# Cross-attention on Trainium2: a rearranged step, and the shift and the subtraction of the maxima as products of 32-row strips

## What is computed

```python
qk = einsum('bhqd,bhkd->bhqk', Q, K)
scores = qk / sqrt(dk)
mean_sim = scores.mean(axis=(-2, -1))
max_sim = scores.max(axis=-1).mean(axis=-1)
probs = softmax(scores)
entropy_proxy = var(probs, axis=-1, ddof=1).mean(axis=-1)
feats = stack([mean_sim, max_sim, entropy_proxy], axis=-1)
hidden = gelu(linear(feats, w1, b1))
hidden = gelu(linear(hidden, w2, b2))
log_t = clip(linear(hidden, w3, b3), log(0.1), log(10))
t = exp(log_t)[..., None]
attn = softmax(qk / (2.0 * t))
return linear(einsum('bhqk,bhkd->bhqd', attn, V), Wo, bo)
```

## Time and profile before

| | us |
|---|---|
| median of 3 runs | 1907.29 (1903.29 to 1908.61) |
| profiled execution | 1907.09 |
| its span, first to last instruction | 1905.3 |
| TensorE busy | 1729.3 (91%) |
| VectorE busy | 1236.1 (65%) |
| ScalarE busy | 923.1 (48%) |
| GpSimd busy | 835.5 (44%) |

### The profile page before, as it was taken

How to read it: one execution, slowest core, us unless ns; L and a number is a source line. 1 busy time by engine, 2 the same in 40 slices (tenths; PEclk the granted TensorE clock), 3 DMA queues, 4 the chain that set the end, 5 groups by cost and what they waited for, 6 DMA issues and landing times. The chain is left out here.

```text
span 1905.3 us, 42459 instructions
## 1 busy us (share of the span) xinstructions
PE 1729.3 (91%) x14484; PEld 1286.7 (68%) x14484; DVE 1236.1 (65%) x2802; ACT 923.1 (48%) x2143; POOL 835.5 (44%) x815
## 2 busy tenths in 40 slices
PE   1999999999947799988999898999699999999998
PEld 0455555555525566666666565555599999999998
DVE  4666666766624566677557666511687777887776
ACT  1455555555423345565556556432455445455543
POOL 1433343344334365666547566411244334444332
PEclk9999999999965578999789898755699999999999
DMA  5000000000000000000000000000000000000000
GB/s 156 2 2 2 1 1 1 1 1 1 2 5 5 4 6 5 6 7 7 5 5 6 5 7 5 2 1 1 1 9 7 8 8 8 8 7 6 8 8 12
DMA packets 26230, 16.50 MB, mean 9 GB/s; under 512 B 6099, under 2 KB 23445, under 8 KB 26133
## 3 DMA queue, kind: packets, MB, share of 16 engines
q1 hardware_dynamic: 26132, 15.23, 2.9%
HBM read 9.97 MB, written 4.19 MB: 7 GB/s over the span
## 5 line engine op out<-in xcount | busy, mean ns | idle before, releaser
L803 ACT ACTIVATE xa_P<-xa_SK 77x1024 f32<-77x1024 f32 x128 | 130.6, 1020 | 161.3 <-PE xa_SK L1088 161.3
L280 ACT ACTIVATE sa_P<-sa_SK 128x1024 f32<-128x1024 f32 x128 | 131.2, 1025 | 147.1 <-PE sa_SK L423 147.1
L246 POOL TENSOR_TENSOR sa_KM<-sa_HQK,sc_headmask 128x512 fp32r<-128x512 f32 x64 | 66.5, 1039 | 292.2 <-ACT sa_HQK L275 292.2
L1361 POOL TENSOR_TENSOR ff_zz<-ff_zt 128x256 f32<-128x256 f32 x32 | 38.3, 1197 | 319.9 <-DVE ff_zt L1558 319.9
L739 POOL TENSOR_TENSOR xa_QMH<-xa_QBH,xc_headmask 128x512 fp32r<-128x512 f32 x64 | 72.0, 1126 | 220.0 <-ACT xa_QBH L795 220.0
L1429 ACT ACTIVATE ff_SG<-bank 128x512 f32<-128x512 f32 x128 | 76.7, 599 | 189.1 <-PE bank L1631 188.9
L1548 DVE TENSOR_TENSOR ff_GL<-ff_GU,ff_GH 128x512 fp32r<-128x512 f32 x128 | 147.4, 1170 | 28.6 <-ACT ff_GH L1434 28.4
L353 DVE TENSOR_REDUCE sa_mx<-sa_SQ 128x8 f32<-128x1024 f32 x128 | 156.6, 1223 | 6.8 <-PE sa_SQ L423 5.4
L1696 PE MATMUL bank<-fh_r,ff_GH 128*128 128x256 f32 x512 | 148.3, 290 | 0.0
L1629 PE MATMUL bank<-ff_ZH,fh_b 128*128 128x256 f32 x512 | 147.7, 288 | 0.0
L1630 PE MATMUL bank<-ff_ZL,fh_b 128*128 128x256 f32 x512 | 144.9, 283 | 0.0
(11 more groups left out here) (254 smaller groups left out, 5430.9 us busy)
## 6 DMA issues: line engine op xcount, KB each, us to landing
xa_shift<-xa_row SPq DMA_DIRECT2D x256, 2.0 KB
out<-X SPq DMA_DIRECT2D x64, 64.0 KB, 1.6
xa_cx<-ctx SPq DMA_DIRECT2D x64, 38.5 KB
sa_shift<-sa_mT SPq DMA_DIRECT2D x64, 8.0 KB, 1.8
fr_b<-L_ffn_B SPq DMA_DIRECT2D x2, 256.0 KB, 3.9
fr_r<-down_a SPq DMA_DIRECT2D x1, 512.0 KB, 4.7
fr_w<-L_ffn_w_gate SPq DMA_DIRECT2D x1, 256.0 KB, 3.4
fr_w<-L_ffn_w_up SPq DMA_DIRECT2D x1, 256.0 KB, 3.6
```

The source lines that it names most:

```text
L280: nc.scalar.activation(P[:, 2 * (k % 2) + h, :], SK[:], ACT.Exp).then_inc(p_ready, 1)
L803: nc.scalar.activation(P[0:TC, (2 * b + h) % 4, :], SK[0:TC, :], ACT.Exp).then_inc(p_ready, 1)
```

## The change

In the part of the cross-attention alone:

- The maxima of the 16 heads are spread over 96 columns (MX: 6 at 0, 6 at 32, 4 at 64), so that mT has the maxima of each bank of SQ in rows of a 32-row group of their own, and subtract_max multiplies 32 rows for each bank.
- The product of pick and shift in by_key takes 32 rows instead of 128. row has 96 partitions and goes to shift by five DMAs (PIECES) instead of four.
- project moves from behind scores_inner to the head of TensorE's step, writes M instead of R, and adds the bias as a product of two fp32r rows (high and low part) with minus ones. residual moves to the head of DVE's step. o_transpose waits for onT_sb of the batch before instead of x_done.
- The MLP writes its three layers into the last quarter of R. POOL makes the features (similarity once a round, variance every second step), DVE the reciprocals (inverse_sums) every second step; the upper clip is done on the exponential. A round's step no longer defers the transposes and qkv of batch n+2; its o_transpose runs behind by_key h = 1 and waits for bounded.
- DVE fills HK, LK, MX and shift; POOL fills ones_row, minus_ones, VA and P, and nobody waits for P before the first exps and pv.

```diff
+    SPREAD = 96
+    PIECES = ((0, 0, 4, 0), (1, 0, 2, 4), (1, 2, 2, 32), (2, 0, 4, 34), (3, 0, 4, 64))
...
-                for g in range(QUADS):
-                    sp.dma_start(shift[32 * g:32 * g + 1, b % 2].bitcast(F32),
-                                 row[JH * g:JH * g + JH].bitcast(F32)).then_inc(m_row[b % 2], 16)
+                for g, j, heads_in, at in PIECES:
+                    sp.dma_start(shift[32 * g:32 * g + 1, b % 2, j:j + heads_in].bitcast(F32),
+                                 row[at:at + heads_in].bitcast(F32)).then_inc(m_row[b % 2], 16)
...
             nc.gpsimd.memset(ones_row[:], 1.0).then_inc(const_set, 1)
-            nc.gpsimd.memset(shift[:].bitcast(F32), 0.0).then_inc(const_set, 1)
-            nc.gpsimd.memset(HK[:].bitcast(F32), 0.0).then_inc(const_set, 1)
-            nc.gpsimd.memset(LK[:].bitcast(F32), 0.0).then_inc(const_set, 1)
-            nc.gpsimd.memset(mT[:].bitcast(F32), 0.0).then_inc(const_set, 1)
+            nc.gpsimd.memset(minus_ones[:].bitcast(F32), -1.0).then_inc(const_set, 1)
             nc.gpsimd.memset(VA[:], 0.0).then_inc(const_set, 1)
...
+            def similarity(r):
+                part = slice(r % 2 * GROUP, r % 2 * GROUP + GROUP)
+                pool.wait_ge(k_sb, GROUP * (r + 1))
+                need(pool, mlp_ps, 3 * (r - 2) + 1)
+                nc.gpsimd.tensor_tensor(qk[:], qsum[:, part], ksum[:, part], ALU.mult).then_inc(qk_ready, 1)
...
+            def variance(i):
...
+                pool.wait_ge(zr_ready, i + 1)
+                pool.wait_ge(z2_done, 2 * i + 2)
+                nc.gpsimd.tensor_tensor(zv[:], ZS[:, 1, cols], zr[:, i % 2], ALU.mult).then_inc(zv_ready, 1)
+                pool.wait_ge(zv_ready, i + 1)
+                nc.gpsimd.tensor_tensor(FEAT[:, 2, cols], zv[:], zr[:, i % 2], ALU.mult).then_inc(var_ready, 1)
...
             for n in STEPS:
                 r = mlp_round(n)
                 if real(n - LAG):
                     exps(n - LAG, 0)
-                if mlp_round(n - 1) is not None and real(n + 1):
-                    qkv_copy(n + 1)
+                if real(n - LAG + 1):
+                    scaled(n - LAG + 1)
+                if real(n + 2):
+                    xcT_copy(n + 2)
                 if r is not None:
                     gelu1(r)
...
+            nc.vector.memset(HK[:].bitcast(F32), 0.0).then_inc(pads, 1)
+            nc.vector.memset(LK[:].bitcast(F32), 0.0).then_inc(pads, 1)
+            nc.vector.memset(MX[:], 0.0).then_inc(pads, 1)
+            nc.vector.memset(shift[:].bitcast(F32), 0.0).then_inc(pads, 1)
...
+            def inverse_sums(i):
...
+                dve.wait_ge(z1_done, 2 * i + 2)
+                need(dve, var_ready, i - 1)
+                nc.vector.reciprocal(zr[:, i % 2], ZS[:, 0, cols]).then_inc(zr_ready, 1)
...
             def subtract_max(b):
                 pe.wait_ge(mT_sb, b + 1)
                 for a, n in enumerate((6, 6, 4)):
-                    last = mm(SQ[:, 512 * a:512 * a + n * TC], mT[:, slot(b)], heads[:, 6 * a * TC:(6 * a + n) * TC],
+                    rows = slice(32 * a, 32 * a + 32)
+                    last = mm(SQ[:, 512 * a:512 * a + n * TC], mT[rows, slot(b)], heads[rows, 6 * a * TC:(6 * a + n) * TC],
                               start=False, stop=True, skip_group_check=True)
...
-                for a, _, r in quads:
-                    mm(bank(SK, a), pick[:, r // 32], shift[:, b % 2].rearrange("c j t -> c (j t)"),
+                for a, rows, r in quads:
+                    mm(bank(SK, a), pick[rows, r // 32], shift[rows, b % 2].rearrange("c j t -> c (j t)"),
                        start=True, stop=False)
...
             def project(b):
                 pe.wait_ge(onT_sb, b + 1)
-                mm(R[:, 3 * T:4 * T], ones_row[:], bias[:], start=True, stop=False)
-                mm(R[:, 3 * T:4 * T], onT[:], wo[:], start=False, stop=True).then_inc(proj_ps, 1)
+                pe.wait_ge(v_sb, min(b + LAG + 4, B))
+                mm(M[:, 0:C], minus_ones[:], bias[:], start=True, stop=False)
+                mm(M[:, 0:C], onT[:], wo[:], start=False, stop=True).then_inc(proj_ps, 1)
...
             for n in STEPS:
                 r = mlp_round(n)
+                if real(n - LAG - 2):
+                    project(n - LAG - 2)
                 if real(n - LAG):
                     by_key(n - LAG, 0)
-                if mlp_round(n - 1) is not None and real(n + 1):
-                    qkv(n + 1)
                 if real(n):
                     scores_outer(n)
+                if real(n - LAG - 1):
+                    pv(n - LAG - 1, 1)
                 if r is not None:
                     mlp1(r, n)
```

More of the change, by code:

```diff
@@ L742, in _ @@
             for n in STEPS:
-                late = mlp_round(n) is not None
-                if mlp_round(n - 1) is not None and real(n + 1):
-                    low(n + 1)
-                    key_masks(n + 1)
+                if n % 2 == 1 and real(n - 2):
+                    variance((n - 3) // 2)
+                if mlp_round(n + 1) is not None:
+                    similarity(mlp_round(n + 1))
                 if real(n - LAG + 1):
@@ L982, in _ @@
                 r = mlp_round(n)
-                if mlp_round(n - 1) is not None and real(n + 1):
-                    cast(n + 1)
-                if r is not None:
-                    features(r)
+                if real(n - LAG - 2):
+                    residual(n - LAG - 2)
+                if n % 2 == 1 and real(n - 2):
+                    inverse_sums((n - 3) // 2)
                 if real(n - 1):
@@ L993, in _ @@
                 if real(n - LAG - 2):
-                    residual(n - LAG - 2)
                     stats(n - LAG - 2)
-                if real(n - LAG - 1):
+                if r is not None:
+                    bound(r)
+                if real(n - LAG - 1) and r is None:
                     norm(n - LAG - 1)
-                if r is not None:
-                    clip(r)
-                if real(n + 2) and r is None:
+                if real(n + 2):
                     cast(n + 2)
+                if r is not None and real(n - LAG - 1):
+                    norm(n - LAG - 1)
                 if real(n - 1):
@@ L1126, in mlp1 @@
+                pe.wait_ge(sim_ready, r + 1)
                 pe.wait_ge(max_ready, 2 * GROUP * (r + 1))
-                pe.wait_ge(v_sb, min(n + 2, B))
-                for f in range(3):
-                    last = mm(M[0:64, 0:128], w1s[:, f, :], of_group(FEAT[:, f], r), start=(f == 0), stop=(f == 2))
-                last.then_inc(mlp_ps, 1)
+                need(pe, onT_sb, n - LAG - 1)
+                hidden = R[0:64, 3 * T:4 * T]
+                by_head = hidden.rearrange("u (s h) -> u s h", h=H)
@@ L1132, in mlp2 @@
+                maxima = MX[:, r % 2 * GROUP:r % 2 * GROUP + GROUP]
+                mm(hidden, w1s[:, 0, :], of_group(FEAT[:, 0], r), start=True, stop=False)
+                for a, n in enumerate((6, 6, 4)):
+                    mm(by_head[:, :, 6 * a:6 * a + n], w1s[:, 1, :], maxima[:, :, 32 * a:32 * a + n], start=False,
+                       stop=False)
+                mm(hidden, w1s[:, 2, :], of_group(FEAT[:, 2], r), start=False, stop=True).then_inc(mlp_ps, 1)
             def mlp2(r):
```

198 lines of the change are left out of this document (104 added, 94 removed).

## The result

The changed kernel takes 2033.47 us (median of 4 executions, 2028.13 to 2039.59) against 1905.29 (4, 1901.14 to 1908.61) for the kernel before on the same chip: ratio 1.0675, interval 1.0637 to 1.0713. It is slower by 6.7%, 128 us. The forecast was 1838 us, and the range ended at 1878. Further down, a slow execution, one more than 1.5% above the fastest of its kernel, is in the median but not in the ratio and its interval.

The account below looks back on a forecast made before the run. Undisturbed cross-attention steps were taken as bound by TensorE in program order with three late waits. Start -8.8, early steps -7.6 and -4, main part -36, tail -13 sum to -69: 1838 us from 1907.29, range 1805 to 1878.

Parts of the forecast that it names:

- with the same 22% at the low level: Main part: low-clock share stays as before, so 430 us of full-clock time become 475 instead of 511, -36 us.
- B: TensorE clock: strips leave less of it active, low share rises to 36%, 1872 us; chance 0.15 together with D.
- C: TensorE clock: same cause as B, slower than before from 49% low level, 1942 us at 60%; chance 0.08.
- (1): Subtraction in strips sharing the array: 0.4 us instead of 0.83, at low level 0.55 instead of 1.40; early steps -0.84 each.
- (2): Shift in 32-row strips in by_key: saves 0.2 us twice a step, between 0.1 and 0.4.
- (3): Project and residual moved: o transposes' 0.84 us wait removed, maxima to next product -0.5; gained is the bias product, -0.15.
- (4): Temperature rounds, first layer's inputs moved to POOL: stall stays 2.9 us, change zero, between -2 and +2 each.
- (5): Shift rows by five DMAs instead of four: 0.6 us more issuing, costs nothing while a cover of 0.4 to 1 us lasts.
- (6): Start of the stage, memsets redistributed: -8.8 us, or -5 if DVE's and POOL's memsets exclude each other.
- (7): Tail, last 12 steps: 9.1 us a step instead of 10.16, -13 us in all (-8 to -22).
- Rival A: DVE and POOL become the bound, casts ending with squares and maxima late: step 8.6 us, 1857 us; chance 0.17.
- Rival D: Strips don't share the array: main step near 8.6, early steps and tail gain little, 1875 us; counted with B, 0.15.

Follow-up runs that it names:

- full shift: Changed kernel with only by_key's shift product in 128 rows again, subtraction still in strips: 1891.01 and 1956.52 us.
- both in full rows: Changed kernel with shift in 128 rows and subtraction in 96 rows again, everything else of the change kept: 1889.18 us, ratio 0.9875.
- full subtraction: Changed kernel with only the subtraction in 96 rows again, shift still in strips: 2086.06 us, ratio 1.0930.

## Why the prediction was wrong

**The step that failed** is in the sum: "with the same 22% at the low level". The main part ran at the low level altogether, 0.50 over 657.9 us, because the strips took away full-row products. I saw the mechanism (rivals B and C) and gave C 0.08, on two grounds that the runs refute. That the main part "came back to full clock after each fall and spent 78% there" was a property of its full-row products, and the change takes rows away from 3280 columns a step: 2048 of the shift, 1232 of the subtraction. That "the emptiest place of its step, the 0.84 us wait, shrinks" weighs busy time, and the control with four 32-row products shows TensorE 100% busy at 0.50. The Trainium skill (TensorE: Matmul & The Clock Gate, HAM oscillation — how this bites in real kernels) puts such falls down to gaps between matmuls; by that rule alone the changed step, busy for 12.74 of its 12.74 us, should have kept its clock. The traces disagree. What should have spoken louder was the tail: already in the kernel before, TensorE was nearly always busy there (83.91 of the last 88.15 us up to the last copy of o), had fewer full-row products than in a main step (no subtraction, no q, k and v, no transposes of x), and was low from end to end.

**The price of the low level** was mis-sized for a stage that is low throughout, on the safe side. I took 0.43 us lost for each low one, from one step with a fall in it. For the falls of the kernel before that was about right: 45 us came back for the 112 that I had reckoned at the low level, 0.40. But whole steps on either level give 8.77 and 13.60 with the full shift, 0.355, and 8.31 (three filler products) and 12.74 (none) with strips, 0.35. With that, my 430 us of full-clock time become 430 / 0.65 = 662; measured 657.9. With 0.43 it would have been 754. The check is a weak one, since 12.74 is itself a step of the measured main part; with the 0.355 of the other kernel it gives 667. So the main part's work was forecast about right, and its time went wrong in one factor, the low share: all of it, not 22%.

Point by point. **(1)** An early step fell from 8.34 to 7.78 us, -0.56 of the -0.84 forecast: the three strips together took 0.75 us at the low level (full: 1.40), not 0.55. All steps up to the second copy of o gave 9.8 us, forecast 7.6 + 4. Against the same kernel with full rows (8.41) the strips alone give -0.63. At the high level in a main step they give 0.12 (8.89 to 8.77), not 0.43. **(2)** The shift in strips gave 0.45 us a step at the high level (8.91 to 8.46, in some steps 8.29), forecast 0.2 twice a step. **(3)** The order alone gives nothing: 8.89 against 8.91. Its parts cancel. The timeline with both in full rows:

```profile
1087.51 1.12 DVE L942 TENSOR_REDUCE xa_MX<-xa_SQ 128x12 f32<-128x924 f32 x1 [0.44 <-PE xa_SQ L1077]
...
1089.14 0.71 PE L1119 MATMUL xa_SK<-xa_shift,xa_pick 128*128 128x512 f32 x2
...
1089.78 0.49 PE L1123 MATMUL xa_SK<-xa_QMH,xa_HK 32*128 32x512 f32 x2
...
1096.42 1.12 DVE L942 TENSOR_REDUCE xa_MX<-xa_SQ 128x12 f32<-128x924 f32 x1 [0.45 <-PE xa_SQ L1077]
```

From maxima to product it is 2.27 us, 0.48 less than before, about the 0.5 of the forecast although that had the strips' shorter shift in it; from product to maxima 6.64, 0.48 more, since project now stands on that way, and only the strips were to pay for that. Together a high-level step with strips took 8.31 us with three filler products in it; 8.25 without any was forecast, so the term of -33 us for 50 steps may be about right. What a step with strips and without filler takes at the high level was never seen. **(4)** A round cost 10.93 + 9.35 - 2 x 8.49 = 3.3 us at the high level and 16.11 + 13.50 - 2 x 12.74 = 4.1 at the low one; forecast 2.9. In the kernel before with filler it costs 10.37 + 10.27 + 9.50 - 3 x 8.91 = 3.4 at the high level, so the forecast of no change between the kernels holds. **(5)** The fifth DMA is free: with four filler products the five issues end at 744.61, and the next first half begins with its shift at 747.17, without a wait. **(6)** The start gave 6.1 us: neither -8.8 nor the -5 for memsets that exclude each other. The memsets did run side by side; what POOL held up were DVE's tensor_scalar and copy. The Trainium skill (SBUF, Who interferes with whom) names copy, cast and tensor_scalar as the DVE operations that can contend with GpSimd for the shared ports, and no memset on this chip; the rows agree, and I had applied the rule to the casts alone. Without that stall it is 8.7. **(7)** A tail step takes 9.19 us, forecast 9.1; the 12 steps gave 8.7 us and not 13, because the first three of them gave 0.3 together (11.66, 11.84 and 11.18 us before, 11.82, 10.86 and 11.66 after) where each was to give 1.06.

Rival A can be put aside: at the high level DVE's row maxima wait for TensorE (0.44 us), not the reverse. Rival D is refuted by the three strips, which take 0.75 us where the three full products took 1.40, and by the early steps.

## What to carry to other kernels

Packing products into 32-row strips saves TensorE time at a given clock, and may cost the clock: count the columns that run over all rows, and if a change takes away much of them, price the whole stage at the low level as well. If a stage sits low although its engine is busy, put full-row products whose result is overwritten into its waits, and read the clock again: four of 512 columns a step turned 2033 us into 1827 here, and the same four in the tail with strips cost 1.7 us a step and lifted nothing. Price a low level from a whole step at it, and look in the kernel itself for a stage that already resembles the one that you are about to make.

## What the runs showed of the hardware

- In these kernels the granted clock follows the rows in use, not the busy time: 0.50 with TensorE busy 99.7% (strips) and 100% (strips and 32-row filler), 0.98 at 96% (strips and full-row filler); in the tail, with four full-row filler products, 1.00 with the shift in 128 rows and 0.50 with it in strips. Zeros count as work: both the shift's operand and the filler's are almost all zero. Whether rows count or cells of the array was not separated.
- With both in full rows the clock of the main part is 0.90: it falls behind each round and comes back one or two steps later. With strips and four full products two falls are left, 0.98, with three more in the rounds' stalls none, 1.00. The full subtraction alone brought nothing back, 0.50.
- The levels differ by less than their ratio of two: a step of 8.77 against 13.60 (full shift), a pair of 32-row products every 0.24 against 0.43 us.
- A memset of POOL held a tensor_scalar and a copy of DVE until it ended (4.09 and 3.81 us against 0.68 and 0.39 without it), but another of 6.71 us ran beside DVE's memsets, and neither was longer for it (6.71 and 1.76 us; one after the other on POOL, 6.71 and 1.79).
